# A mixture-of-experts layer on TensorE: the experts' products of 512 columns written as two of 256

## The reference, cut to what matters

```
gate_logits = softmax(x @ gate_w + gate_b)
selected = (gate_logits >= 0.1)
weights = gate_logits * selected          # then divided by their sum
for e in range(8):
    out = out + weights[:, e:e+1] * (x @ expert_w[e] + expert_b[e])
x = x + gb * out
```

## Time and profile before

| | |
|---|---|
| median of 3 timed runs | 2198.18 us (2197.79 to 2201.4) |
| the profiled execution, from its first to its last instruction | 2195.2 us |
| TensorE, products / loads busy | 2138.3 us (97%) / 1781.6 us (81%) |
| VectorE, ScalarE, GpSimd busy | 80%, 80%, 77% |
| mean granted TensorE clock | 0.992 of full speed |

### The profile page before, as it was taken

The page is one execution under the profiler, slowest core; times in us unless marked ns, Lnnn a source line. Parts: engine busy times, 40 slices in busy tenths (PEclk is TensorE's granted clock), DMA queues, the critical chain, the costliest instruction groups (busy, mean ns, idle before and its releaser), DMA issues.

```text
span 2195.2 us, 51248 instructions
## 1 busy us (share of the span) xinstructions
PE 2138.3 (97%) x16090; PEld 1781.6 (81%) x16090; DVE 1761.4 (80%) x4001; ACT 1750.8 (80%) x4402; POOL 1682.2 (77%) x1812
## 2 busy tenths in 40 slices
PE   6799999999999999999999999999999999999997
PEld 5678888888888888888888888888888888888875
DVE  7778778887778888788888788888788887788863
ACT  5788887888887888888888888888888888888872
POOL 3568787777787777787777787777787777787786
PEclk9899999999999999999999999999999999999998
DMA  4221222222222222222222222222212222222210
GB/s 138 88 78 52 83 62 66 88 79 64 83 62 67 88 79 63 83 62 67 88 75 67 83 62 67 88 74 68 83 62 67 88 70 72 80 65 67 78 56 20
DMA packets 152204, 161.03 MB, mean 73 GB/s; under 512 B 15128, under 2 KB 134528, under 8 KB 151936
## 3 DMA queue, kind: packets, MB, share of 16 engines
q1 hardware_dynamic: 150160, 157.63, 23.4%
q10 hardware_dynamic: 1776, 0.12, 0.1%
HBM read 139.88 MB, written 17.83 MB: 72 GB/s over the span
## 4 chain that ended last, share of the span: by engine, by line
PE 89%; issue 3%; POOL 3%; DVE 3%; ACT 2%; DMA 0%; POOLq 0%; SPq 0%; DVEq 0%; ACTq 0%
PE pe L1320 32%; PE pa L1320 22%; PE pd L1320 12%; PE px L1320 10%; PE py L1320 6%; PE px L1432 3%; PE pa L1338 1%; PE pd L1491 1%; DVE feat L933 1%; PE py L1423 1%; POOL xd L423 0%; POOL ex L474 0%; POOL ex L479 0%; POOL ex L485 0%; POOL ex L470 0%
## 5 line engine op out<-in xcount | busy, mean ns | idle before, releaser
L933 DVE SCALAR_TENSOR_TENSOR feat<-pa,cw,feat 128x512 f32<-128x512 f32 x567 | 423.8, 747 | 83.5 <-ACT feat L609 73.1
L1320 PE MATMUL pe<-e_hi,h_hi 128*128 128x512 f32 x1024 | 443.7, 433 | 3.7 <-DVE eacc L1124 2.0
L1320 PE MATMUL pe<-e_lo,h_hi 128*128 128x512 f32 x1024 | 405.2, 396 | 0.0
L1320 PE MATMUL pe<-e_hi,h_lo 128*128 128x512 f32 x1024 | 404.4, 395 | 0.0
L1320 PE MATMUL pa<-h_hi,w_hi 128*128 128x260 f32 x1260 | 371.8, 295 | 6.3 <-DVE feat L933 5.7
L1320 PE MATMUL pa<-h_hi,w_lo 128*128 128x260 f32 x1260 | 357.8, 284 | 0.0
L1320 PE MATMUL pa<-h_lo,w_hi 128*128 128x260 f32 x1260 | 357.0, 283 | 0.0
L681 ACT ACTIVATE lm<-lm,lndt 128x128 f32<-128x128 f32 x1024 | 329.7, 405 | 2.5
L671 ACT ACTIVATE lm<-lm,e3in 128x128 f32<-128x128 f32 x1024 | 324.6, 405 | 1.1 <-DMA lm<-cs_rows 1.1
L761 ACT ACTIVATE ex<-pe,wg 128x256 f32<-128x256 f32 x512 | 215.0, 478 | 114.7 <-PE pe L1320 93.1
L1124 DVE SCALAR_TENSOR_TENSOR eacc<-pe,wg,eacc 128x256 f32<-128x256 f32 x512 | 244.3, 477 | 31.8 <-PE pe L1320 22.8
(11 more groups left out here) (184 smaller groups left out, 5659.3 us busy)
## 6 DMA issues: line engine op xcount, KB each, us to landing
lm<-cs_rows SPq DMA_DIRECT2D x128, 512.0 KB, 4.0
ebc<-cs_rows SPq DMA_DIRECT2D x256, 128.0 KB, 3.6
xin<-_attn_hidden_states_dram SPq DMA_DIRECT2D x32, 512.0 KB, 5.1
xres<-_attn_hidden_states_dram SPq DMA_DIRECT2D x128, 128.0 KB, 3.7
out_dram<-x SPq DMA_DIRECT2D x128, 128.0 KB, 3.9
gz<-in_L_wmod_dram SPq DMA_DIRECT2D x2, 512.0 KB, 8.2
ex<-in_L_ffn_expert_w_dram SPq DMA_DIRECT2D x1, 1024.0 KB, 11.5
x<-in_L_ffn_expert_w_dram SPq DMA_DIRECT2D x1, 1024.0 KB, 13.9
```

The source lines that it names most:

```text
L933: dve.scalar_tensor_tensor(out=acc, in0=proj_bank(x, i)[:, :, 1 + j:1 + j + HT], scalar=cw[:, f, j:j + 1], in1=acc, op0=ALU.mult, op1=ALU. ...
L1320: return pe.matmul(o, lhsT=l, rhs=r, start=start, stop=stop, skip_group_check=True)
```

## The change

In the expert steps the one call of `split` for 512 columns becomes two, for the 256 columns of the first expert and then for the 256 of the second. In `before` a step is 6 loads and 6 products of 512 columns, in the changed kernel 12 loads and 12 products of 256 columns. The stationary operand of each is the same as before, and loaded once for each half. The waits stand ahead of the first product and the increment behind the last, as before.

```diff
-                    last = split(pe_[:, i % 2], lambda k: h2_hi[:, x.pair % NH2, k, x.half], lambda k: h2_lo[:, x.pair % NH2, k, x.half],
-                                 e_hi, e_lo, slice(2 * i * DM, 2 * (i + 1) * DM))
+                    for e in range(2):
+                        last = split(pe_[:, i % 2, e * DM:(e + 1) * DM], lambda k: h2_hi[:, x.pair % NH2, k, x.half],
+                                     lambda k: h2_lo[:, x.pair % NH2, k, x.half], e_hi, e_lo, slice((2 * i + e) * DM, (2 * i + e + 1) * DM))
                     last.then_inc(S["expA" if i % 2 else "expD"], 1)
```

## The result

The changed kernel takes 2203.27 us in the median of 17 runs (2197.99 to 2205.92), the kernel before 2198.37 us in 17 (2196.16 to 2201.4). The ratio is 1.0021, 95% interval 1.0014 to 1.0027: slower by 4.9 us, with 3.1 to 5.9 us in the interval. The sum of the prediction gave 10.9 us more, the stated time of 2208 us 9.8. The sign was right, and the size is half of the stated one and less than half of the sum.

The account below looks back on a forecast made before the run. TensorE's stream of products was taken as the bound. 3.7 ns x 2950 pairs = +10.9 us on 2198.18 gave 2209.1, stated as 2208 us; the forecast's own range was 2203 to 2213, the 8-in-10 range 2186 to 2224.

Parts of the forecast that it names:

- What bounds the kernel: Mid-kernel, TensorE's stream of products sets the pace; some 2950 of the experts' 3072 products lie on the deciding path.
- The one number decides: In the experts, all depends on twice the distance of a 256-column product, with its load, against 232.5 ns.
- I take the line: +3.7 ns for each pair: Experts follow the z projection's rate, 118.1 ns per 256 columns: 3.7 ns x 2950 = +10.9 us; chance 0.40.
- The prediction's own sign: In the changed kernel's chain, `pe` pieces of 24 products should take 2.83 us where 12 took 2.79.
- No term for others: DVE and ACT start emptying banks as before, moved only by 22 ns a step; the projections' pieces keep their times.
- The loads keep 5 to 8 ns of room: In the experts, a load of 110 ns still hides under a product of 118 ns; no term added.
- Rival B: The experts' loads show: a pair takes 240.0 ns, +7.5 ns, +22 us in all, 2220 us; chance 0.18.
- Loads' busy time is no wall: TensorE's load durations would total 2362 us in a span of 2195, harmless because loads overlap each other.
- First products, waits, clock, instructions: Step openings add nothing, TensorE's bank waits stay a few us, clock unchanged, 0.4 MB more instructions cost nothing.
- Rival C: Experts run at 116.3 to 117 ns, a pair costing -1 to +1 ns: 2195 to 2201 us; chance 0.12.
- Rival A: Expert pairs run as the output projection does, -5.2 to -2.5 ns each: 2183 to 2191 us, faster; chance 0.25.
- Rival D: In the experts, each load carries the whole excess over the clock: +19.2 ns a pair, +57 us, 2255; chance 0.05.

Follow-up runs that it names:

- h2_aligned_before: The kernel before with the experts' stationary operands h2_hi and h2_lo moved by 32 bytes in SBUF, to offset 0; 2189.29 us, ratio 0.9955.
- h2_aligned_after: The changed kernel with the experts' stationary operands h2_hi and h2_lo moved by 32 bytes in SBUF, to offset 0; 2214.52 us, ratio 1.0071 to the kernel before.
- uneven288: The changed kernel with each expert step split into products of 288 and 224 columns instead of 256 and 256; 2230.08 us, ratio 1.0146 to the kernel before.
- again_before: The kernel before, unchanged, profiled a second time; 2198.29 us.

## Why the prediction was right and wrong, point by point

- *What bounds the kernel.* Right. What 31 turns of TensorE gain or lose, the time gains or loses: 8.0 and 9.5 us (h2_aligned_before), 15.6 and 16.1 (h2_aligned_after), 30.9 and 31.6 (uneven288).
- *The one number decides.* Right in the main: the experts' term is 3.3 us of a change of 4.0. The two streams that the trace offered as models disagreed, and the text said so.
- *"I take the line: +3.7 ns for each pair".* This is the step that failed. The experts run at 116.7 ns and not at 118.1, and by the sums over 28 turns a pair costs 1.1 ns more than one product of 512. In the sum, 3.7 ns x 2950, this is the term that was mis-sized. A line through the z projection's products and the experts' mixes two streams with different operands, and its fixed part of 3.7 ns is not a price of a product: on the experts' own operands the price of the split goes from -1.6 to 23.6 us in 31 turns with the offset alone. The argument "half of 232.5 is 116.3, above the 113.6, so no gain" also fell: at offset 64 pairs of steps run at 113.6. That the sign came out right is this offset's doing, and so luck: at 64 the split saves 1.6 us in 31 turns, and the times show no difference (2197.26 and 2197.03). The prediction's own sign said so: its line asked for pieces of 24 in 2.83 us, and they take 2.80 and 2.81.
- *No term for others.* Incomplete. The output projection, which the prediction left alone, adds some 1.8 us (0.055 us a turn times 32), and small gains elsewhere take 1.1 back. again_before and the stretches of x22 show that it is an effect of the change. By what way stays open.
- *The loads keep 5 to 8 ns of room.* Right: the floor is 111 to 112 ns (uneven288). Rival B did not occur.
- *Loads' busy time is no wall.* Right as to the time; the forecast of 2360 us was wrong, 1939.9: it added 581 us of durations to a busy time in which overlapping loads count once.
- *First products, waits, clock, instructions.* Right: TensorE's wait for `eacc` is still 2.0 us, the clock 0.992.
- *Rival C* (116.3 to 117 ns, a pair -1 to +1 ns) came nearest: 116.7 ns, +1.1. Its upper end of 2201 us was passed by about what the output projection added.
- *Rival A* (pairs as the output projection) is real at the output projection's own offset, in part of the steps. *Rival D* needed 125.9 ns; the slowest offset gave 120.

Of the forecast 10.9 us, the experts' term came to 3.3 (1.08 ns x 3072), the unforeseen one to 1.8. That 2203.27 lies just inside the forecast's own range of 2203 to 2213 is luck too: without the second it would have been some 2201.5.

## What to carry to other kernels

Where two streams of one shape run at different distances in a trace, ask what differs in their operands before taking one as the model of a third: here the offset between the stationary and the moving tile modulo 256 bytes was worth 6.5 ns in a pair of 256-column products (23.700 us a turn at 64, 24.322 at 0, for 96 pairs), six times what the edit cost. Before judging an edit to a stream of products by a fraction of a per cent, try both versions at several places of their tiles; a pad of 32 bytes took the kernel before down by 0.5%. And do not make a product shorter than its load: 224 columns paid the load's 111 ns, where 256 still took their own 113 to 120.

## What the runs showed that I had not expected

- Streams of these products fall into fixed paces, and one stream of the same form can stand at either of two in the same trace: 113.3, 117.5 and 120 ns for 256 columns, and a cycle of 114, 116, 117 and 120; 226.7 and about 233 for 512. The load beside a product is what I suppose the stream meets, since only its place against the stream's counts. That is argued, not shown: no run has products without loads.
- The pace of a step can be handed on. The output projection takes 1.94 us in one stretch of before and 1.96 or 1.99 in the changed kernel with its own operands untouched. By what it is handed on stays open.
- 31 turns of one program repeat to 0.1 us between executions, while the time ahead of them was 136.2 and 138.5 us in two executions of one kernel. The granted clock goes with it: 0.91 and 0.89 in the first 136 us, 1.00 from there to 2150 us in both. It goes with the timed runs too: of the 17 of the changed kernel the four with a mean clock of 0.990 took 2204.35 to 2205.92 us, and the one with 0.995 took 2197.99. So most of their spread seems to be the clock of the launch and of the end, and has nothing to do with either form of the experts.
